# The shared expert as steps of the expert pipeline, and the routing of two batches drawn together

## The reference

```python
normed = layernorm(x) * ln_gamma + ln_beta
logits = normed @ router_w.T                       # 8 experts
probs = softmax(logits)
top_v, top_i = top_k(probs, 2)
gates = softmax(top_v)
comb = sum(one_hot(top_i, 8) * gates[..., None])
out = sum_e comb[:, e] * swiglu(normed, gate_up_w[e], down_w[e])   # hidden width 384
out = out + swiglu(normed, shared_gate_up_w, shared_down_w)        # hidden width 128
x = x + tanh(g_ffn[1]) * out
```

## Time and profile before

| | us |
|---|---|
| median of 3 runs | 330.95 (329.2 to 334.0) |
| the profiled execution | 331.9 |
| its span, first to last instruction | 330.1 |
| TensorE busy in the span | 275.3 (83%) |
| VectorE, ScalarE, POOL busy | 236.2, 205.2, 159.3 |
| mean granted clock of TensorE | 0.915 |

### The profile page before, as it was taken

One profiled execution on the slowest core, in us unless ns is written; L12 is line 12 of the kernel. 1 busy time (PEld: TensorE's weight loads), 2 busy tenths in 40 slices (PEclk: granted clock), 3 DMA queues, 4 the chain that ended last, 5 costly groups with the idle time before them and its releaser, 6 DMA issues.

```text
span 330.1 us, 7523 instructions
## 1 busy us (share of the span) xinstructions
PE 275.3 (83%) x2406; PEld 206.1 (62%) x2406; DVE 236.2 (72%) x715; ACT 205.2 (62%) x472; POOL 159.3 (48%) x206
## 2 busy tenths in 40 slices
PE   7878977978998869998898525587799999999942
PEld 3553523556776547876676411366599999999942
DVE  3585398847878648789899677935376767767786
ACT  2865899875676688768646533213467676665570
POOL 2534394035425285260137777700017888878631
PEclk9999998999999999999987555958699999999995
DMA  7890003003399999800001111120122322201074
GB/s 204 224 356 21 3 0 127 2 1 128 98 183 184 194 175 188 141 0 2 1 18 34 36 41 57 49 67 0 26 67 62 90 68 74 65 31 40 2 223 127
DMA packets 34612, 28.12 MB, mean 85 GB/s; under 512 B 3072, under 2 KB 32389, under 8 KB 33936
## 3 DMA queue, kind: packets, MB, share of 16 engines
q1 hardware_dynamic: 32192, 23.77, 32.0%
q0 software_dynamic: 2240, 3.72, 3.5%
q10 hardware_dynamic: 144, 0.15, 0.3%
HBM read 14.15 MB, written 14.40 MB: 87 GB/s over the span
## 4 chain that ended last, share of the span: by engine, by line
PE 36%; DVE 27%; issue 13%; POOL 12%; ACT 6%; DMA 3%; SPq 1%; POOLq 0%; DVEq 0%; ACTq 0%
PE bank L1211 31%; POOL expert_rows L851 11%; DVE region_k L918 2%; DVE top L917 2%; DMA region_q<-expert_rows 2%; DVE x L1167 1%; DVE bn_raw L876 1%; DMA wq<-in 1%; DVE region_x L1180 1%; PE bank L1435 1%; DVE nm L1006 1%; DVE region_k L1008 1%; DVE x L908 1%; ACT x_hat L535 1%; DVE region_k L975 1%
## 5 line engine op out<-in xcount | busy, mean ns | idle before, releaser
L1211 PE MATMUL bank<-w_high,region_k 128*128 (+1 forms) x380 | 39.7, 227 | 14.4 <-DVE x L1194 8.9
L1199 DVE TENSOR_TENSOR region_k<-region_x,region_k 128x768 f16<-128x768 f32 x29 | 27.8, 958 | 26.6 <-ACT region_k L723 26.6
L851 POOL DMA_INDIRECT expert_rows<-region_k,slot_dest x22 | 27.1, 1232 | 39.4 <-DVE region_k L1190 32.1
L1211 PE MATMUL bank<-w_scaled,w_high 128*128 128x256 f16 x252 | 44.1, 279 | 0.9 <-ACT w_scaled L709 0.9
L1211 PEld LDWEIGHTS bank<-w_high,region_k 128*128 128x128 f16 x380 | 32.0, 102 | 16.8 <-issue 9.3
L825 POOL DMA_INDIRECT dispatched_rows<-region_t,slot x28 | 28.6, 1021 | 16.4 <-issue 8.3
L1211 PE MATMUL bank<-w_low,region_k 128*128 (+1 forms) x190 | 35.7, 227 | 0.0
L1211 PE MATMUL bank<-w_scaled,w_low 128*128 128x256 f16 x126 | 35.1, 278 | 0.0
L1180 DVE SCALAR_TENSOR_TENSOR region_x<-bank,region_w 128x768 f32<-128x768 f32 x29 | 27.6, 953 | 6.4 <-PE bank L1211 3.2
L723 ACT ACTIVATE region_k<-region_x 128x768 f16<-128x768 f32 x29 | 24.3, 837 | 10.0 <-DVE region_x L1180 10.0
L1211 PE MATMUL bank<-filler 128*128 128x512 f16 x94 | 26.9, 407 | 3.9 <-DVE region_k L918 2.4
(11 more groups left out here) (244 smaller groups left out, 750.7 us busy)
## 6 DMA issues: line engine op xcount, KB each, us to landing
dispatched_rows<-pad_rows SPq DMA_DIRECT2D x8, 1048.0 KB, 18.9
w_scaled<-in SPq DMA_DIRECT2D x5, 1024.0 KB, 8.3
w_scaled<-dispatched_rows SPq DMA_DIRECT2D x21, 131.0 KB, 2.3
region_q<-expert_rows SPq DMA_DIRECT2D x3, 512.0 KB, 5.1
x<-in SPq DMA_DIRECT2D x4, 256.0 KB, 4.6
region_w<-in SPq DMA_DIRECT2D x2, 512.0 KB, 6.9
out<-x SPq DMA_DIRECT2D x3, 256.0 KB, 2.3
w_scaled<-in SPq DMA_DIRECT2D x1, 704.0 KB, 4.0
```

Of the source, the lines that this page charges most:

```text
L851: pool.indirect_dma_start(ytok, bass.IndirectOffsetOnAxis(dst[:, n, h:h + 1].bitcast(U32), 0), yv[n % 4][:, h * D:(h + 1) * D], None, boun ...
L1199: dve.tensor_tensor(hsplit[:, v, HB:2 * HB], hid[:, v, :], hsplit[:, v, 0:HB], ALU.subtract).then_inc(hidden_low, 1)
L1211: return pe.matmul(o, l, r, start=start, stop=stop)
```

## The change

- The shared expert's four batches become steps of kind `shared` ahead of the dense ones in `STEPS`, with the same queues, buffers and bank 7 for all results; each uses 512 columns where the others use 768. The banks of gate and up go by a small table. Its first gate_up waits only for the end of cross attention, the second for the slots, the third for the logits to have been read.
- Two dense experts, not three, stand ahead of the rows; six behind them.
- The two largest and their indices are taken from the logits in PSUM. The exponentials are done once for all tiles at the end; the work after them is `top2_apart`, behind the first hidden product. The gates come from tanh of half the difference, in place of exponential and reciprocal.
- In the loop, the routing stages of tiles 3 and 7 get slots of their own.
- `turn(0)` stands ahead of down at the step before the first rows step.
- Two small tiles (`ge`, `gn`) move to another buffer, which adds a wait for `w_low_done`. At the end the row sums of batches 0 and 1 are split by tile, and the orders of loads and stores differ.

```diff
-DENSE_FIRST = 3
-STEPS = [("dense", e) for e in range(DENSE_FIRST)] + [("rows", n) for n in range(TILES)] + [("dense", e) for e in range(DENSE_FIRST, E)]
+DENSE_FIRST = 2
+STEPS = [("shared", b) for b in range(B)] + [("dense", e) for e in range(DENSE_FIRST)] + [("rows", n) for n in range(TILES)] + [("dense", e) for e in range(DENSE_FIRST, E)]
+GATE_BANK = {0: 2, 1: 0, 2: 4}
...
+C_PE_AT = {("turn", 3): 11.3, ("logits", 3): 11.8, ("rank", 3): 12.6, ("turn", 7): 15.3, ("logits", 7): 15.8, ("rank", 7): 16.6,
...
+C_ACT_AT = {("norm2", 3): 10.2, ("high", 3): 10.9, ("turn_out", 3): 11.7, ("norm2", 7): 14.2, ("high", 7): 14.9, ("turn_out", 7): 15.7,
...
+C_DVE_AT = {("affine", 3): 10.7, ("low", 3): 11.1, ("route", 3): 12.2, ("slots", 3): 12.8, ("affine", 7): 14.7, ("low", 7): 15.1, ("route", 7): 16.2, ("slots", 7): 16.8,
...
-C_POOL_AT = {("rstd2", 13): 19.4, ("rstd2", 15): 21.5, ("send2", 7): 21.6, ("send", 11): 21.7, ("send2", 11): 21.8, ("send", 13): 21.9}
+C_POOL_AT = {("send2", 3): 14.4, ("send", 3): 13.0, ("send", 7): 17.0,
+             ("rstd2", 13): 19.4, ("rstd2", 15): 21.5, ("send2", 7): 18.4, ("send", 11): 21.7, ("send2", 11): 21.8, ("send", 13): 21.9}
...
-        ge, gn = (xf[:, i * TTAB * E:(i + 1) * TTAB * E].rearrange("p (s e) -> p s e", e=E) for i in (2, 3))
+        ge, gn = (wf[:, (8 + i) * CH:(8 + i) * CH + TTAB * E].rearrange("p (s e) -> p s e", e=E) for i in range(2))
...
+        def gate_up_bank(s):
+            return GATE_BANK.get(s, 3 * ((s + 1) % 2))
...
-            for g in (2, 0, 3, 1):
+            for g in (0, 2, 1, 3):
                 eng.dma_start(yk[:, n, :], ytok_v[:, n, :]).then_inc(x_loaded[g], 16)
...
+            act.wait_ge(logits_read, len(GROUPS))
+            act.activation(prob[:, :, :], prob[:, :, :], ACT.Exp, scale=1.0 / WS)
+            act.activation(ptop[:, :, :], ptop[:, :, :], ACT.Exp, scale=1.0 / WS).then_inc(route_exp, 1)
             nc.scalar.preload_act_table(ACT.Silu)
...
+                if s == 0:
+                    act.wait_ge(top2_difference, 1)
+                    act.activation(gone[:, :], gdif[:, :], ACT.Tanh, scale=0.5).then_inc(top2_tanh, 1)
...
                 elif stage == "route" and g is not None:
                     dve.wait_ge(route_logits, g + 1)
+                    for u in range(w):
+                        last = dve.max(rtop[:, lo + u, :], l3[:, u, :])
                     link(last)
                     for u in range(w):
+                        last = dve.max_index(ridx[:, u, :], rtop[:, lo + u, :], l3[:, u, :])
+                    if g == SPARSE:
+                        dve.tensor_tensor(ptop[:, :, :], rtop[:, :, 0:2], rtop[:, :, 0:1].to_broadcast((P, NT, 2)), ALU.subtract)
+                    last = dve.tensor_tensor(prob[:, n, :], l3, rtop[:, n, 0:1].to_broadcast((P, w, E)), ALU.subtract)
+                    last.then_inc(logits_read, 1)
+                    dve.wait_ge(logits_read, g + 1)
...
+            def top2_apart():
+                dve.wait_ge(route_exp, 1)
+                link(dve.tensor_reduce(rsum[:, :], prob[:, :, :], AX.X, ALU.add))
+                link(dve.reciprocal(rsum[:, :], rsum[:, :]))
+                link(dve.tensor_tensor(ptop[:, :, :], ptop[:, :, :], bc(rsum[:, :], 2), ALU.mult))
+                dve.tensor_tensor(gdif[:, :], ptop[:, :, 1], ptop[:, :, 0], ALU.subtract).then_inc(top2_difference, 1)
...
+            dve.wait_ge(w_low_done, CHUNKS)
             tiles_counted()
-            between = {1: tiles_placed, 2: windows_packed, 3: gates_of_all}
+            after_hidden = {0: top2_apart, 1: tiles_placed, 2: windows_packed, 3: gates_of_all}
...
             for s in range(len(STEPS) + 2):
...
+                if s in after_hidden:
+                    after_hidden[s]()
...
+                    elif kind == "shared":
+                        dve.scalar_tensor_tensor(xf32, bank[7][:, :], tgw[:, :], xf32, ALU.mult, ALU.add).then_inc(rows_ready, 1)
...
                 if s == len(STEPS) - 1:
-                    sum_rows(0)
+                    sum_rows(range(0, 1))
                 elif s == len(STEPS):
-                    sum_rows(1)
+                    sum_rows(range(1, 4))
+            dve.wait_ge(x_loaded[1], 32)
+            sum_rows(range(4, 8))
...
                 if s == 0:
-                    pe.wait_ge(sh_hidden, B)
+                    pe.wait_ge(cross1_exp_out, NT)
+                    pe.wait_ge(cross1_over_sum, NT)
                 elif s == 1:
-                    pe.wait_ge(sh_added, B)
+                    pe.wait_ge(slots_ready, SPARSE)
+                elif s == 2:
+                    pe.wait_ge(logits_read, len(GROUPS))
...
                 if late:
-                    down(s - 1, None)
                     pe.wait_ge(tiles, 2)
...
                     turn(0)
+                    down(s - 1, None)
```

More of the change, by code:

```diff
@@ L89 @@
 C_ACT = {"early_chunk": -4.9, "keys_out": -4.8, "last_key_out": -1.95, "first_norm": -1.9, "chunk": -1.15, "norm": 1.1, "xt_out": 1.8, "exp": 3.2, "e1t": 4.5, "ont": 6.5, "norm2": 8,
-         "high": 8.6, "turn_out": 10.8, "exp_logits": 11.4}
+         "high": 8.6, "turn_out": 10.8}
 C_DVE = {"residual": -4.8, "shift": 1.9, "over_sum": 4.4, "add": 6.3, "affine": 7.6, "low": 8.9,
-         "shift_logits": 10.4, "route": 10.9, "slots": 12}
+         "route": 10.9, "slots": 12}
 C_POOL = {"rstd": -4.6, "early_low": -5.3, "low": -0.9, "rstd2": 6.5, "send": 12.5, "send2": 16.1}
@@ L94 @@
 C_FIRST = 3
-C_PE_AT = {("turn", 11): 19.95, ("logits", 11): 20.6, ("turn", 13): 21.2, ("logits", 13): 21.4, ("rank", 11): 21.5,
+C_PE_AT = {("turn", 3): 11.3, ("logits", 3): 11.8, ("rank", 3): 12.6, ("turn", 7): 15.3, ("logits", 7): 15.8, ("rank", 7): 16.6,
+           ("turn", 11): 19.95, ("logits", 11): 20.6, ("turn", 13): 21.2, ("logits", 13): 21.4, ("rank", 11): 21.5,
            ("turn", 15): 22.2, ("logits", 15): 22.5, ("rank", 13): 22.6}
-C_ACT_AT = {("turn_out", 11): 20.55, ("norm2", 13): 20.7, ("high", 13): 20.9, ("exp_logits", 11): 21.55, ("turn_out", 13): 21.6,
-            ("norm2", 15): 21.9, ("exp_logits", 13): 22.0, ("high", 15): 22.1, ("turn_out", 15): 22.3, ("exp_logits", 15): 22.5}
@@ L99 @@
-C_DVE_AT = {("affine", 13): 20.8, ("shift_logits", 11): 20.9, ("low", 13): 21.0, ("route", 11): 21.4, ("slots", 11): 21.6,
-            ("shift_logits", 13): 21.8, ("affine", 15): 22.0, ("low", 15): 22.1, ("route", 13): 22.2, ("shift_logits", 15): 22.4,
+C_ACT_AT = {("norm2", 3): 10.2, ("high", 3): 10.9, ("turn_out", 3): 11.7, ("norm2", 7): 14.2, ("high", 7): 14.9, ("turn_out", 7): 15.7,
+            ("turn_out", 11): 20.55, ("norm2", 13): 20.7, ("high", 13): 20.9, ("turn_out", 13): 21.6,
+            ("norm2", 15): 21.9, ("high", 15): 22.1, ("turn_out", 15): 22.3}
@@ L101 @@
+C_DVE_AT = {("affine", 3): 10.7, ("low", 3): 11.1, ("route", 3): 12.2, ("slots", 3): 12.8, ("affine", 7): 14.7, ("low", 7): 15.1, ("route", 7): 16.2, ("slots", 7): 16.8,
+            ("affine", 13): 20.8, ("low", 13): 21.0, ("route", 11): 21.4, ("slots", 11): 21.6,
+            ("affine", 15): 22.0, ("low", 15): 22.1, ("route", 13): 22.2,
             ("route", 15): 22.5, ("slots", 13): 22.9}
-C_POOL_AT = {("rstd2", 13): 19.4, ("rstd2", 15): 21.5, ("send2", 7): 21.6, ("send", 11): 21.7, ("send2", 11): 21.8, ("send", 13): 21.9}
+C_POOL_AT = {("send2", 3): 14.4, ("send", 3): 13.0, ("send", 7): 17.0,
+             ("rstd2", 13): 19.4, ("rstd2", 15): 21.5, ("send2", 7): 18.4, ("send", 11): 21.7, ("send2", 11): 21.8, ("send", 13): 21.9}
@@ L294, in build @@
         xt_ps = bank[6][:, 0:TP].bitcast(F16)
-        gu_ps = [psum[:, v * 3 * 512:(v + 1) * 3 * 512] for v in range(2)]
         yv = [region_k[:, 3, r * TP:(r + 1) * TP] for r in range(2)] + [xf[:, 2 * HB + r * TP:2 * HB + (r + 1) * TP] for r in range(2)]
@@ L1041, in _ @@
                                       ALU.subtract).then_inc(ffn_low, 1)
-                elif stage == "shift_logits" and g is not None:
+                elif stage == "route" and g is not None:
                     l3 = bank[TURN_BANK[g][0]][:, 0:w * E].rearrange("p (t e) -> p t e", e=E)
                     dve.wait_ge(route_logits, g + 1)
-                    link(dve.tensor_reduce(rmax[:, 0:w], l3, AX.X, ALU.max, negate=True))
-                    dve.tensor_tensor(prob[:, n, :], l3, bc(rmax[:, 0:w], E), ALU.add).then_inc(route_shifted, 1)
-                elif stage == "route" and g is not None:
-                    dve.wait_ge(route_exp, g + 1)
-                    for u in range(lo, hi):
-                        last = dve.max(rtop[:, u, :], prob[:, u, :])
+                    for u in range(w):
+                        last = dve.max(rtop[:, lo + u, :], l3[:, u, :])
                     link(last)
@@ L1586, in expert_of @@
                 kind, n = STEPS[s]
-                if kind == "dense":
+                if kind != "rows":
                     return None
```

170 lines of the change are left out of this document (57 added, 113 removed).

## The result

Times are medians in us; ratios are to runs of the kernel before on the same chip, with a 95% interval. A few runs fall in a slower state with a lower granted clock; they count in the medians and not in the ratios, so the two can differ by up to 0.6%.

A forecast was written before the change was run, and what follows sets the result against it. Bounds: VectorE in the loop, short dependent chains and mutual waits after it, then TensorE in the steady pipeline. From 330.1, +19.2 - 10.1 = +9.1 and +2.8 give span 342.0, so 343 against the median; range 338 to 346.

The forecast's parts named there:

- Item 1: Loop, batch 0: norm2 now ahead of the next tile's exponential; add of tile 4 at 151.3, VectorE idle 3.3 us.
- Item 2: Loop, batch 0: turn_out ahead of tile 10's xt_out on ScalarE waits for turn; VectorE dry 3.0 us.
- Item 3: Loop, batch 1: four sends hold rstd 3.7 us on POOL, norm2 also moves ahead; VectorE's waits 9.2 us.
- Item 5: Loop, batch 2: rstd waits for batch 1's sends again, 3.7 us; VectorE's waits before affine and earlier sum to 5.7 us.
- Sum of the loop: Loop: 23.0 us of waits against 1.3 before, work the same within 0.1 us; last add at 204.9.
- The shared expert and the dense steps: First shared gate_up to second rows step: 26.7 us instead of 36.8, a gain of 10.1.
- The tail: After the last rows step: six dense steps, not five, and sums after the last down; +2.8 us in all.
- A: Rival: the loop's waits are covered and it ends where it did; 320 us, faster; chance 0.15.
- B: Rival: only part of the loop's waits appear, 5 to 18 us; 325 to 338, no clear change; chance 0.29.
- D: Rival: shared expert in one pipeline gains nothing, stretch stays 36.8 less 3.0; 350 us; chance 0.06 together with C.
- C: Rival: TensorE falls to 1.2 GHz more often, in loop and first rows steps; 347 to 351; chance 0.06 together with D.
- Items 2 and 4: Loop: turn_out queued ahead of xt_out and waiting for turn, VectorE idle 3.0 us in batch 0, 1.8 in batch 1.

## Why the prediction was right

The mechanism and most of its terms held. By its own steps, with 2.6 us added to each time of the prediction for the later start:

- **Item 1, norm2 of batch 0**: the add of tile 4 at 151.3 + 2.6 = 153.9; measured 153.94. The run that moves norm2 alone shows it too: the waits for `x` go, though not the time.
- **Item 2, turn_out**: slots of batch 0 end at 166.2 + 2.6 = 168.8; measured 169.4. For the 3.0 us of VectorE's idle time two waits of `nm` stand in the trace, 1.27 and 2.09, but only the second is turn_out's. The first, at 158.44, ends before turn_out runs (160.87); ahead of it TensorE, at a granted clock of 0.76 from 154 to 161 us, took 1.70 us for the scores.
- **Item 3, rstd of batch 1 behind four sends**: forecast 3.7 us held and the add of tile 8 at 8.8 us after the statistics; measured 3.3 and 8.4. (The walk lets four sends last 5.1 and 5.2 us, by its own row they take 5.0.) Taking the sends back moved the first gate_up 6.1 us forward. Two batches at 3.3 us each make 6.6.
- **Item 5, batch 2**: 5.5 us of idle before affine forecast; in the trace 5.0 in three waits (2.76 of affine, 1.30 of the add, 0.93 of z_inv). Slots of batch 1 end at 195.4 forecast, 196.3 measured.
- **Sum of the loop**: 23.0 us of VectorE's waits against 23.3, last add at 204.9 + 2.6 = 207.5, near the end of that work in the trace (207.8). The prediction took 1.3 us for the kernel before and left out 0.5 of affine (1.8 by the view). That the sum is so near is partly luck: the walk used old durations, with 0.3 us in the loop for the lower clock, while the clock fell from 0.89 to 0.76.
- **First shared gate_up** at 222.9 forecast, 222.61 measured. The sends end at 234.9 in both.
- **The shared expert and the dense steps**: the mechanism was right and its size was off: 26.7 us forecast, 24.6 measured. The failing term is VectorE's 14.4 us from the first hidden values to low of the last shared step; measured 12.2. (VectorE began 0.4 us later than forecast, and the steps behind gained 0.6 more.)

```profile
225.54:237.74 12.20, 9.07 (x62) 5.94 (x61) 11.61 (x34) 4.64 (x9) 7.24 (x8) 0.83 0.16 47
```

  I had added 1.4 us of gaps between 38 instructions. Hardly any are there: in 12.20 us VectorE is busy 11.61, and 0.2 us of the rest is a wait. Rows of one engine can even overlap by some 0.08 us (an instruction of 0.69 us at 225.54 is followed by one at 226.15). The five small instructions that count the tiles also ran ahead of the first hidden values, at 224.34 to 225.33, where I had them inside.
- **The tail**: +2.8 forecast, +2.6 measured.
- **The tanh**: no table was loaded for it. It runs in 205 ns between two Silus, and the program has two table loads in all. So 0 us, as I took it. The groups of table loads, and the timeline at the tanh (L728):

```profile
L534 ACT ACT_TABLE_LOAD x1 | 1.3, 1283 | 1.2 <-PEq L1661 1.2
L700 ACT ACT_TABLE_LOAD x1 | 1.3, 1283 | 0.0
```

```profile
226.80 0.58 ACT L723 ACTIVATE region_w<-bank 128x512 f32<-128x512 f32 x1
227.28 0.20 ACT L728 ACTIVATE second_share<-top_difference_of 128x16 f32<-128x16 f32 x1
```

The Trainium skill (ScalarE: Activation LUTs, Table sets: the hidden batching unit) lists tanh beside exp and names Silu in no set. Read as if the two were in different sets, that gave the prediction's estimate of up to 2.4 us more. The trace doesn't bear this reading out, no load stands between Silu and tanh.

- **The rivals**: A (waits covered, 320) and B (5 to 18 us of waits) are out, with 23.3 us in the trace. D (one pipeline gains nothing) is out: 33.8 us by it from the first gate_up to the second rows step, measured 24.6. C's slower clock is there in part (0.76 over the loop, scores of 1.70 to 1.91 us), inside the sum; the first rows steps ran at 1.00.

What the prediction missed is the second half of the cause. Items 2 and 4 (turn_out) were walked as waits of one moved instruction, 4.8 us together. Yet with norm2 and the sends back and turn_out a place further on, 12.9 of the 23.1 us stay, and with all stages a tile later 11.3. How they divide between high, turn, turn_out and the routing on VectorE is open: they wait for each other through the queues, TensorE's lower clock lengthens each wait, and they were not moved one at a time to their old places.

## What to carry to other kernels

When several engines work through one written order, a moved stage costs what stands behind it in its queue until its data come. Before drawing a chain of stages together, lay the hand-over times (here POOL 1.9, norm2 1.65, affine, copy, turn, copy) beside the distance between their slots, and check that no instruction with free data (here rstd, exponentials, the attention copies) is queued behind one that waits. Allow also for TensorE's clock: here the loops with 11 us of waits and more had 0.67 to 0.83, the one with 1.8 had 0.92, and a wait at the start of the rows cost its own length and 1.4 to 1.7 us more in the step behind it. VectorE's busy share of 91% was not proof that latency didn't matter: it was the state in which all latency was covered, and it fell to 59% at once. And test a bundle by its parts: this one was 4% slower because one part lost 6% and the others gained 2%, and with one more dense step in front those others gain 3.4%.
